# A low-rank product that contracts over 64 rows, two tiles side by side in TensorE

## The reference

```python
# x: (8, 512, 2048) f32
x = x + einsum('bsi,boi->bso', x, L0_weight[ids0])             # one of 8 adapters, 2048 x 2048 each
base   = einsum('bti,oi->bto', x, W) + b                       # shared W, 2048 x 2048
lora_h = einsum('bti,bir->btr', x, lora_As[ids1])              # rank 16, one of 32 adapters
lora   = einsum('btr,bro->bto', lora_h, lora_Bs[ids1])
x = x + base + lora * 2.0
```

## Time and profile before

| | before |
|---|---|
| executions | 2563.78 us median, 2563.7 to 2566.4 us, n = 3 |
| profiled execution | 2562.13 us, its span 2560.6 us |
| TensorE (PE) busy | 2553.9 us, 11246 matmuls |
| TensorE weight loads (PEld) busy | 2112.2 us |
| VectorE (DVE) busy | 1666.0 us |
| ScalarE (ACT) busy | 875.7 us |
| GpSimd (POOL) busy | 1251.4 us |
| granted TensorE clock | 1.00 over the whole span |

### The profile page before, as it was taken

One profiled execution on the slowest core, in us unless ns is written; L12 is line 12 of the kernel. 1 busy time (PEld: TensorE's weight loads), 2 busy tenths in 40 slices (PEclk: granted clock), 3 DMA queues, 4 the chain that ended last, 5 costly groups with the idle time before them and its releaser, 6 DMA issues.

```text
span 2560.6 us, 31029 instructions
## 1 busy us (share of the span) xinstructions
PE 2553.9 (100%) x11246; PEld 2112.2 (82%) x11246; DVE 1666.0 (65%) x1885; ACT 875.7 (34%) x1161; POOL 1251.4 (49%) x1471
## 2 busy tenths in 40 slices
PE   9999999999999999999999999999999999999999
PEld 7888888888888888888888888888888888888887
DVE  5445455454354454364443368999998689999995
ACT  4232232232232232232322234343343343333333
POOL 3434434443454334334323466556666655556655
PEclk9999999999999999999999999999999999999999
DMA  9998888998999887899977887457777855546764
GB/s 340 330 302 295 299 285 282 299 285 281 272 297 336 269 290 273 261 292 284 295 190 196 223 310 265 139 173 251 266 240 254 292 168 175 155 150 203 238 224 143
DMA packets 238939, 648.03 MB, mean 253 GB/s; under 512 B 30148, under 2 KB 46532, under 8 KB 238788
## 3 DMA queue, kind: packets, MB, share of 16 engines
q0 software_dynamic: 123440, 393.28, 48.2%
q1 hardware_dynamic: 115060, 252.24, 30.6%
q10 hardware_dynamic: 288, 0.52, 0.1%
HBM read 433.07 MB, written 212.86 MB: 252 GB/s over the span
## 4 chain that ended last, share of the span: by engine, by line
PE 98%; DMA 1%; SPq 0%; DVE 0%; issue 0%; POOL 0%; POOLq 0%; DVEq 0%
PE bank L914 42%; PE bank L856 18%; PE bank L857 18%; PE bank L858 18%; PE bank L845 1%; PE bank L929 1%; PE bank L846 1%; DMA q_raw<-w1T 1%; DMA ids_sb<-ids 0%; SPq L299 0%; SPq L313 0%; DVE q_raw L712 0%; DVE w_lo L667 0%; POOL q_raw L402 0%; POOLq L375 0%
## 5 line engine op out<-in xcount | busy, mean ns | idle before, releaser
L914 PE MATMUL bank<-xc,wl 128*128 128x512 f32 x4704 | 1087.6, 389 | 0.1
L914 PEld LDWEIGHTS bank<-xc,wl 128*128 128x128 f32 x4704 | 882.9, 188 | 183.7 <-issue 0.5
L856 PE MATMUL bank<-x_hi,w_hi 128*128 128x512 f32 x2048 | 797.1, 389 | 0.9 <-DVE w_lo L667 0.9
L429 POOL TENSOR_TENSOR wl<-wl 128x512 fp32r<-128x512 f32 x392 | 599.5, 1548 | 406.0 <-ACT wl L593 404.4
L857 PE MATMUL bank<-x_lo,w_hi 128*128 128x512 f32 x2048 | 796.8, 389 | 0.0
L858 PE MATMUL bank<-x_hi,w_lo 128*128 128x512 f32 x2048 | 796.7, 389 | 0.0
L547 ACT ACTIVATE w_hi<-w_raw 128x1024 fp32r<-128x1024 f32 (+1 forms) x260 | 258.4, 1039 | 969.5 <-PE bank L858 964.4
L777 DVE TENSOR_TENSOR x_raw<-bank,x_raw 128x512 f32<-128x512 f32 x128 | 88.5, 691 | 693.5 <-PE bank L858 634.5
L856 PEld LDWEIGHTS bank<-x_hi,w_hi 128*128 128x128 f32 x2048 | 384.4, 188 | 82.1 <-DVE w_lo L667 2.0
L858 PEld LDWEIGHTS bank<-x_hi,w_lo 128*128 128x128 f32 x2048 | 384.4, 188 | 79.9
L857 PEld LDWEIGHTS bank<-x_lo,w_hi 128*128 128x128 f32 x2048 | 384.4, 188 | 79.7
(11 more groups left out here) (44 smaller groups left out, 1262.8 us busy)
## 6 DMA issues: line engine op xcount, KB each, us to landing
w_raw<-w0T SPq DMA_DIRECT2D x252, 512.0 KB, 7.7
wl<-w1s SPq DMA_DIRECT2D x392, 256.0 KB, 2.9
xss<-x_raw POOLq DMA_DIRECT2D x256, 256.0 KB, 4.5
w1s<-q_raw POOLq DMA_DIRECT2D x196, 256.0 KB, 7.3
q_raw<-w1T POOLq DMA_DIRECT2D x96, 512.0 KB, 9.8
xq<-xss POOLq DMA_DIRECT2D x40, 1024.0 KB, 6.9
x1s<-x_raw POOLq DMA_DIRECT2D x128, 256.0 KB, 2.9
c<-x1s POOLq DMA_DIRECT2D x32, 1024.0 KB, 7.0
```

Source lines behind the costliest of these rows:

```text
L429: pool.tensor_tensor(w[:, 1], w[:, 1].bitcast(F32), w[:, 0].bitcast(F32), ALU.subtract).then_inc(wl_ready, 1)
L856: pe.matmul(sums[s][:], w_hi[s][:, k, :], x_hi[:, k, :], start=(k == 0), stop=False)
L914: mm = pe.matmul(bank[m][:], w[:, w_part, k, :], x[:, x_part, k, :], start=(p == 0 and k == 0 and BEGIN[j]), stop=(p == 2 and k == Q - 1), ...
```

## The change

The 8 blocks of 16 rows become 4, in 64 rows: low part of B with the high part of h; high part of B with h from the low part of A, with the low part of h, and with its high part. The 128 rows of `bm` and `hm` hold this twice: for `bm` rows 0 to 63 belong to one output tile and 64 to 127 to the next; `hm` repeats the same 64 rows. Two matmuls of 64 rows each, in rows 0 to 63 and 64 to 127 of the array, replace two of 128. Both stand after the tiles with odd `m`, and VectorE adds both there. `bm` is loaded once for two tiles. In stage one, `a_mix` gets two more high copies from ScalarE and two fewer low parts from VectorE, `h_lo` writes 16 rows in place of 32, `b_lo` is two instructions of 16 rows in place of one of 64, and `store_b` two DMAs in place of one. What the 128-row form added beyond these four products (low times low) is left out.

```diff
     NG = P // (2 * R)
+    A_HI = NG + NG // 2
+    ROWS = P // 2
...
-    bs = scratch("bs", (NB, 2, P, HALF * P))
+    bs = scratch("bs", (NB, 2, HALF // 2, P, P))
...
-            def load_bm(i):
-                b, o = low_rank_place(i)[0:2]
-                sp.dma_start(bm[i % BM][:].bitcast(F32), bs[b, o // HALF, :, o % HALF * P:(o % HALF + 1) * P]
-                             ).then_inc(bm_loaded[i % BM], 16)
+            def load_bm(pair):
+                b, o = low_rank_place(2 * pair)[0:2]
+                sp.dma_start(bm[pair % BM][:].bitcast(F32), bs[b, o // HALF, o % HALF // 2]
+                             ).then_inc(bm_loaded[pair % BM], 16)
...
-                    if old is not None:
+                    if old is not None and (n - WL) % 2 == 1:
                         i = old + (n - WL) % Q
                         sp.wait_ge(low_rank_done, i + 1)
-                        if i + BM < 2 * LOW:
-                            load_bm(i + BM)
+                        if i // 2 + BM < LOW:
+                            load_bm(i // 2 + BM)
...
             def store_b(b, half):
-                pool.wait_ge(b_ready, 2 * b + half + 1)
-                pool.dma_start(bs[b, half], b_mix[:].bitcast(F32)).then_inc(b_stored, 16)
+                pool.wait_ge(b_ready, (2 * b + half + 1) * 2)
+                for i in range(2):
+                    rows = slice(i * ROWS, (i + 1) * ROWS)
+                    pool.dma_start(bs[b, half, :, rows].rearrange("q p n -> p q n"),
+                                   b_mix[rows, :].bitcast(F32).rearrange("p (q i n) -> p q i n", i=2, n=P)[:, :, i]
+                                   ).then_inc(b_stored, 16)
...
                 for g in range(NG):
                     act.activation(a_mix[:, :, g, 0:R], a_raw[:], ACT.Copy).then_inc(a_hi_done, 1)
+                for g in range(1, NG, 2):
+                    act.activation(a_mix[:, :, g, R:2 * R], a_raw[:], ACT.Copy).then_inc(a_hi_done, 1)
...
             def a_lo(b):
-                for g in range(NG):
-                    dve.wait_ge(a_hi_done, b * NG + g + 1)
+                dve.wait_ge(a_hi_done, (b + 1) * A_HI)
+                for g in range(0, NG, 2):
...
-                dve.scalar_tensor_tensor(out=b_mix[P // 2:P, :], in0=b_raw[P // 2:P, :], scalar=LORA_SCALING,
-                                         in1=b_mix[P // 2:P, :].bitcast(F32), op0=ALU.mult,
-                                         op1=ALU.subtract).then_inc(b_ready, 1)
+                for first in range(0, P, ROWS):
+                    rows = slice(first, first + R)
+                    dve.scalar_tensor_tensor(out=b_mix[rows, :], in0=b_raw[rows, :], scalar=LORA_SCALING,
+                                             in1=b_mix[rows, :].bitcast(F32), op0=ALU.mult,
+                                             op1=ALU.subtract).then_inc(b_ready, 1)
...
-                    if first_low is not None:
+                    if first_low is not None and m % 2 == 1:
                         dve.wait_ge(acc_free, s * Q + m + 1)
-                        add_low_rank(first_low + m, bank_y[m])
+                        for place in (m - 1, m):
+                            add_low_rank(first_low + place, bank_y[place])
...
-                    if first_low is not None:
+                    if first_low is not None and m % 2 == 1:
...
-                        pe.wait_ge(bm_loaded[i % BM], (i // BM + 1) * 16)
-                        pe.matmul(bank_y[m][:], bm[i % BM][:], hm[i // NT % 2][:], start=True, stop=True
-                                  ).then_inc(low_rank_done, 1)
+                        pair = i // 2
+                        pe.wait_ge(bm_loaded[pair % BM], (pair // BM + 1) * 16)
+                        for half in range(2):
+                            rows = slice(half * ROWS, (half + 1) * ROWS)
+                            pe.matmul(bank_y[m - 1 + half][:], bm[pair % BM][rows], hm[i // NT % 2][rows],
+                                      start=True, stop=True).then_inc(low_rank_done, 1)
```

More of the change, by code:

```diff
@@ L345, in _ @@
                     if n == 2 * WL:
-                        sp.wait_ge(b_stored, NB * 2 * 16)
+                        sp.wait_ge(b_stored, NB * 4 * 16)
                         for i in range(BM):
@@ L380, in load_b @@
                 if 2 * b + half > 0:
-                    pool.wait_ge(b_ready, 2 * b + half)
+                    pool.wait_ge(b_ready, (2 * b + half) * 2)
                 slot = pool.value_load(ids_sb[0:1, 1, b:b + 1], min_val=0, max_val=SLOTS - 1)
@@ L466, in _ @@
                     if t == 3 and b < NB - 1:
-                        pool.wait_ge(a_ready, (b + 1) * NG)
+                        pool.wait_ge(a_ready, (b + 1) * (NG // 2))
                         load_a(b + 1)
@@ L508, in _ @@
                     pool.wait_ge(h_stored, NB * 16)
-                    pool.wait_ge(b_stored, NB * 2 * 16)
+                    pool.wait_ge(b_stored, NB * 4 * 16)
                     for i in range(2):
@@ L570, in b_hi @@
                 if b + half > 0:
-                    act.wait_ge(b_stored, (2 * b + half) * 16)
+                    act.wait_ge(b_stored, (2 * b + half) * 2 * 16)
                 act.activation(b_mix[:], b_raw[:], ACT.Copy, scale=LORA_SCALING).then_inc(b_hi_done, 1)
@@ L684, in h_lo @@
                 for g in range(1, NG, 2):
-                    rows = slice(g * 2 * R, (g + 1) * 2 * R)
+                    rows = slice(g * 2 * R, g * 2 * R + R)
                     dve.tensor_tensor(h_mix[rows, :], h_sum[rows, :], h_mix[rows, :].bitcast(F32),
@@ L840, in add_h @@
                 if t == 0:
-                    pe.wait_ge(a_ready, (b + 1) * NG)
+                    pe.wait_ge(a_ready, (b + 1) * (NG // 2))
                     if b > 0:
```

## The result

The change makes the kernel slower: 2575.93 us median (2574.56 to 2577.16, 6 runs) against 2564.25 us (2563.48 to 2566.4, 6 runs), a ratio of 1.0045 with a 95% interval of 1.0034 to 1.0056, or 11.7 us. The profiled execution has a span of 2574.5 us, 13.9 us over that of before.

A forecast was written before the change was run, and what follows sets the result against it. TensorE's matmul slots of 0.2267 us were taken as the bound; -7.5 us from the pairs, with 0 for switches and VectorE's order, gave 2554.6 us profiled, 2556.3 us against the median; 8-in-10 range 2549 to 2585 us.

The forecast's parts named there:

- The bound: Whole kernel: time goes by TensorE's matmul slots, 0.2267 us each in the dense stretch, with weight loads hidden.
- Two matmuls of 64 rows for two of 128: Low-rank pairs: second matmul starts 0.11 us after the first, a pair takes 0.337 us, 7.5 us saved over 64.
- the first rival: Low-rank pairs: both loads come early, a pair takes one slot, 14.5 us saved, 2549.6 us in all; chance 0.20.
- Going from 128 rows to 64 and back: TensorE around each pair, 128 times: taken as 0; upper end 0.326 us a pair, 20.9 us, plus exposed loads.
- break-even of 0.06 us: TensorE's row switches: the price of one switch above which the forecast gain turns into a loss (0.117/2).
- the rivals in which it drains: TensorE finishes what is in flight at switches: loads not waiting 0.16, loads included 0.18, pair one after the other 0.08.
- the cases in which switches cost next to nothing: TensorE's pairs without a switch price: the forecast 0.28, both loads early 0.20, not side by side 0.10.
- The switches drain, loads included: TensorE's pairs: tails and three loads exposed, 27.5 us lost, 2591.3 us; with two loads 20.4, 2584.2 us; chance 0.18.
- the one whose loads do not wait: TensorE's pairs: switches expose the tail only, 0.553 us a pair, 6.4 us lost, 2570.1 us; chance 0.16.
- VectorE's new order: Low-rank additions of even tiles move behind the next accumulation: 0 to 1 us of TensorE's waits, taken as 0.
- The tight place: Step after a low-rank one with j = 5: TensorE waits for bank_y[0] some 0.1 us, up to 0.5 us.
- Stage one: Copies, subtractions, b_lo and stores of stage one: added work hidden, the one a_mix wait perhaps 0.2 us shorter.

The follow-up runs named there:

- e2: The changed kernel with the second matmul of each pair left out; 2574.05 us, 1.0040 of the kernel before.
- e3: The changed kernel with both matmuls of a pair in the same rows, 0 to 63; 2590.30 us, 1.0101 of the kernel before.
- e9: The kernel before with its 128 single low-rank matmuls over rows 0 to 63 only, no pairs; 2614.01 us, 1.0193 of the kernel before.
- e5: The kernel before with its 128 single low-rank matmuls over rows 0 to 95 only; 2566.50 us, 1.0012 of the kernel before.
- e1: The changed kernel with each matmul of a pair over all 128 rows, so none of 64; 2563.05 us, 1.0001 of the kernel before.
- e4: The changed kernel with a step's four low-rank matmuls, and VectorE's four additions, together behind tile m = 1: 32 stretches for 64; 2562.88 us, 0.9997 of before.
- e8: The changed kernel with a step's four low-rank matmuls side by side in 32 rows each, low parts of h and B left out; 2556.33 us, 0.9972 of before.
- e7: The kernel of e4 with VectorE's additions two behind tile m = 1 and two behind m = 3; 2564.62 us, 1.0006 of the kernel before.

## Why the prediction was wrong

**The bound, right.** TensorE was busy for 2553.9 us of the 2560.6 of before and was 98% of its chain, so a slot taken from it or added to it is time. It is 97 to 99% of the chain that ended last in every run, and a slot is 0.2267 us.

**"Two matmuls of 64 rows for two of 128", right in kind, too small.** I let the second matmul start 0.11 us behind the first, because no row showed a load two ahead. The two loads start 0.003 us apart, the matmuls 0.004; e2 and e3 show that the second is nearly free in other rows (0.030 us) and costs a slot in the same ones. The gain is the full slot of the first rival, 14.5 us, less 1.9 us for those 0.030, and not 7.5. My inference went from loads into the same rows to loads into different rows, which the rows of before could not bear out.

**"Going from 128 rows to 64 and back", the step that failed: I took 0.** The reason given, that loads and matmuls overlap whatever they write, came from a trace in which nothing was ever divided. Measured, a switch is 0.20 us: 0.09 us after the last slot in which nothing starts, and 0.11 us of a load in the open. Two are 0.40 us (e9), so each is over three times the break-even of 0.06 us in my own sum; even against the full slot saved, that would be 0.11 each. So the ledger of 64 pairs is 14.5 us saved, 25.6 us paid for the switches and 1.9 us for the second matmuls: 13.0 us lost, where I had forecast 7.5 us gained. At each change from 128 rows to 64 or back nothing, not even a load, starts for 0.09 us; around the matmuls of 96 rows (e5) no distance between starts is more than 0.010 us wider than a slot. What TensorE does in the 0.09 us no trace shows. I gave the rivals in which it drains 0.42 in all, less than the 0.58 of the cases in which switches cost next to nothing, and neither had a measurement behind it.

**"The switches drain, loads included", the rival that happened, mis-sized.** It gave 27.5 us, or 20.4 with two loads exposed; stage two lost 12.6. Two terms were off: I priced the drain at the record's tail, 0.163 us, where 0.09 is exposed (a record's end is modelled, and the bound stood for more than it could show), and I counted three loads one after the other, where the pair's two load together, so that two are exposed. With these: 0.2267 + 0.18 + 0.22 = 0.627 us a pair, 0.17 more than 0.453, 11.1 us; the starts gave 0.180 and 11.5. The median of 2575.93 us lies between this rival and the one whose loads do not wait. It lies inside my range only because the rivals had stretched that.

**VectorE's new order, right.** 0 us counted, no wait of TensorE found, and e1 is level. The tight place I walked through had no wait. When four additions stood together (e4), the wait that came was for the split of the right operand, not for the bank.

**Stage one, right as to the change.** The distance between the two starts around the first use of `a_mix` went from 0.53 to 0.30 us, the 0.2 us that I had foretold; `b_lo` took 38.8 us on VectorE in place of 19.6 and hid. The 1.4 us at the third tile are the scatter of a DMA, as the old stage one shows it too: VectorE waited 7.54 us for the data of that sum in the changed kernel, and 6.17 (before), 6.72 (e5) and 7.34 us (e9) with the old stage one.

## What to carry to other kernels

Matmuls of 64 or 32 rows in different rows of the array ran together here, loads too (starts 0.003 us apart), but a stretch of them inside a stream of 128-row matmuls cost 0.40 us (e9), 1.8 slots of 512 columns, and did so with one (e9), two (the change) or four matmuls in it (e4, e8). So count stretches, not matmuls: one that saved a single slot lost (the change, 11.7 us), one that saved two broke even (e4 and e7, ratios of 0.9997 and 1.0006), one that saved three gained (e8, 7 us); gather the small matmuls, or use blocks small enough that four go at once. And when a step's price is in no row of the trace, the value that suits the sum deserves no more than the ones against it.

## What the hardware showed that I had not expected

- Two loads of 64 rows (the change), or four of 32 (e8), in different rows start 0.003 to 0.004 us one after the other and together take the time of one, 0.19 us.
- A switch is the same to 64 rows (the change) and to 32 (e8): 0.32 us to the first load, 0.43 us from there to the next of 128 rows.
- A matmul of 96 rows causes no switch (e5), but the four distances from its start on are 0.026 us wider together, 3.3 us over 128 of them; behind pairs of 64 rows it is 0.023 us a pair (the change), behind single matmuls of 64 rows nothing (e9). I have no cause for it.
